# A recurrent attention kernel: keys and queries in three rounded passes, the state's halves made by GpSimd

## The reference

```python
q = _phi((h @ wq + bq_).reshape(b, s, H, DH))      # phi(t) = elu(t) + 1
k = _phi((h @ wk + bk_).reshape(b, s, H, DH))
v = (h @ wv + bv_).reshape(b, s, H, DH)
kv = jnp.einsum('bshd,bshm->bhdm', k, v)
z = 1.0 / (jnp.einsum('bshd,bhd->bsh', q, k.sum(axis=1)) + 1e-06)
att = jnp.einsum('bshd,bhdm,bsh->bshm', q, kv, z).reshape(b, s, d)
h = _ln(h + att @ wo + bo_, g1_, be1_)
y = jax.nn.gelu(h @ w1 + c1_, approximate=False) @ w2 + c2_
h = _ln(h + y, g2_, be2_)
```

## Time and profile before

| | |
|---|---|
| median of 3 runs | 879.8 us (879.21 to 880.77) |
| the profiled execution's own time | 876.81 us |
| its span | 875.1 us |
| TensorE busy | 835.1 us (95%), weight load 772.6 (88%) |
| VectorE busy | 799.0 us (91%) |
| ScalarE busy | 716.4 us (82%) |
| GpSimd busy | 394.6 us (45%) |
| mean granted clock | 0.973 |
| chain that ended last | PE 83%, DVE 10%, issue 3%, ACT 3% |

### The profile page before, as it was taken

The page is one execution under the profiler, slowest core; times in us unless marked ns, Lnnn a source line. Parts: engine busy times, 40 slices in busy tenths (PEclk is TensorE's granted clock), DMA queues, the critical chain, the costliest instruction groups (busy, mean ns, idle before and its releaser), DMA issues.

```text
span 875.1 us, 19581 instructions
## 1 busy us (share of the span) xinstructions
PE 835.1 (95%) x6170; PEld 772.6 (88%) x6170; DVE 799.0 (91%) x2698; ACT 716.4 (82%) x1271; POOL 394.6 (45%) x355
## 2 busy tenths in 40 slices
PE   6799999999999999999999999999999999988876
PEld 5598999999999999999999999999999999877663
DVE  6989999998899989999899989989899989999998
ACT  3589999989998899989998899989998889756443
POOL 5244454445445454445445455454545455432113
PEclk9899999999999999999999999999999999999885
DMA  4300101010010101010010101010010000000002
GB/s 145 88 1 2 43 1 35 1 43 2 1 34 2 43 2 34 2 43 1 1 34 2 43 2 34 1 43 1 2 34 1 2 1 1 17 10 1 1 0 98
DMA packets 26265, 18.79 MB, mean 21 GB/s; under 512 B 4354, under 2 KB 22195, under 8 KB 26164
## 3 DMA queue, kind: packets, MB, share of 16 engines
q1 hardware_dynamic: 25300, 16.95, 6.8%
q10 hardware_dynamic: 864, 0.59, 0.2%
HBM read 15.43 MB, written 2.10 MB: 20 GB/s over the span
## 4 chain that ended last, share of the span: by engine, by line
PE 83%; DVE 10%; issue 3%; ACT 3%; DMA 0%; ACTq 0%; DVEq 0%
PE down_ps L742 23%; PE att_ps L706 7%; PE small_ps L676 6%; PE k_ps L661 6%; PE q_ps L668 6%; PE up_ps L732 5%; PE up_ps L734 5%; PE up_ps L733 5%; PE t_ps L651 3%; PE t_ps L713 3%; PE up_ps L697 3%; PE small_ps L684 2%; PE k_ps L732 2%; PE k_ps L734 2%; PE small_ps L685 2%
## 5 line engine op out<-in xcount | busy, mean ns | idle before, releaser
L742 PE MATMUL down_ps<-w_use,hid 128*128 128x128 f32 x2048 | 263.5, 278 | 0.7 <-ACT hid L845 0.7
L742 PEld LDWEIGHTS down_ps<-w_use,hid 128*128 128x128 f32 x2048 | 247.6, 195 | 1.9 <-ACT hid L845 1.1
L1005 POOL TENSOR_TENSOR res_ffn<-z_tm,g_ffn 128x512 f32<-128x512 f32 x64 | 102.1, 1595 | 216.3 <-DVE z_tm L983 216.3
L995 POOL TENSOR_TENSOR res_att<-z_tm,g_att 128x512 f32<-128x512 f32 x64 | 82.6, 1291 | 204.7 <-DVE h L948 204.7
L845 ACT ACTIVATE hid<-up_ps 128x512 f32<-128x512 f32 x192 | 113.7, 592 | 20.5 <-PE up_ps L734 12.1
L960 DVE BATCH_NORM_STATS2 st<-h 128x6 f32<-128x128 f32 x512 | 108.9, 274 | 0.1
L900 ACT ACTIVATE z_tm<-h,shift,rstd 128x128 f32<-128x128 f32 x224 | 92.4, 483 | 0.7
L1008 POOL TENSOR_TENSOR res_ffn<-res_ffn,ffn_row 128x512 f32<-128x512 f32 x64 | 85.5, 1335 | 5.0
L732 PE MATMUL up_ps<-z_hi,w_hi 128*128 128x512 f32 x192 | 86.8, 452 | 0.3 <-DVE z_lo L988 0.3
L894 ACT ACTIVATE z_hi<-t_ps 128x512 fp32r<-128x512 f32 x64 | 38.1, 596 | 58.1 <-PE t_ps L713 58.1
L1058 DVE SCALAR_TENSOR_TENSOR q_ks<-q_elu,small_ps 128x512 f32<-128x512 f32 x64 | 43.9, 686 | 43.6 <-PE small_ps L685 43.0
(11 more groups left out here) (188 smaller groups left out, 1891.7 us busy)
## 6 DMA issues: line engine op xcount, KB each, us to landing
raw_w<-in_L_attn_W SPq DMA_DIRECT2D x15, 256.0 KB, 4.2
out_y<-gate_tm SPq DMA_DIRECT2D x8, 256.0 KB, 2.2
bias_bc<-in_L_attn_c SPq DMA_DIRECT2D x7, 256.0 KB, 4.5
x_tm<-in_L_attn_x SPq DMA_DIRECT2D x3, 512.0 KB, 6.6
raw_rows<-in_L_attn_be SPq DMA_DIRECT2D x15, 64.0 KB, 4.2
raw_g<-in_L_attn_g SPq DMA_DIRECT2D x14, 64.0 KB, 3.1
x_tm<-in_L_attn_x SPq DMA_DIRECT2D x2, 256.0 KB, 3.3
raw_rows<-in_L_attn_bo SPq DMA_DIRECT2D x8, 64.0 KB, 3.9
```

The costliest lines, as they stand in the source:

```text
L742: last = nc.tensor.matmul(down_ps[:, t, :], hid[:, j, t * P:(t + 1) * P], w2_use[:, j, :], start=(j == 0), stop=(j == FC - 1))
L1005: nc.gpsimd.tensor_tensor(res_ffn[:, b % 2, :, :], z1_tm[:, :, :], g_ffn[:, :].unsqueeze(1).to_broadcast([P, TT, D]), ALU.mult).then_inc(s ...
```

## The change

Keys and queries of one unit share one matmul with 256 columns, keys left and queries right: the weights stand in the order K, Q (`w_kq`), the loads of weights and biases change places accordingly, and the result goes to `kq_ps`, two PSUM banks with two tiles each. The product is made as in the up matmuls, of rounded halves: three fp32r passes per tile, 12 per unit, for the 4 + 4 float32 matmuls of before. Since the second bank is also the place of the third up chunk, that chunk waits for `q_elu_s` as well, and the keys' phi on VectorE waits for `qrel`.

The halves of the state, `zq_hi` and `zq_lo`, are made by GpSimd from `z_fm` (one buffer now) at the head of its period, ahead of both residuals. To have the state earlier, TensorE transposes it before attention, and ScalarE copies it before the second norm. For the first two units ScalarE and VectorE make the halves from PSUM. `pool_qk` splits the weights into halves likewise. `pool_res_ffn` has a further wait on `tk`.

```diff
-        q_ps = ps("q_ps", [P, TT, D])
-        k_ps = ps("k_ps", [P, TT, D])
+        kq_ps = ps("kq_ps", [P, TT, 2, D])
+        k_ps, q_ps = kq_ps[:, :, 0, :], kq_ps[:, :, 1, :]
...
         def pool_qk(pool, l):
             pool.wait_ge(s["fold_a"], l)
-            pool.wait_ge(s["qproj"], l * SEQS)
-            pool.wait_ge(s["kproj"], l * SEQS)
+            pool.wait_ge(s["kqproj"], l * SEQS)
             pool.sem_inc(s["pool_waited"], 1)
-            nc.gpsimd.tensor_copy(w_qk[:, :], fold_att[:, 0:2 * D]).then_inc(s["qk_ready"], 1)
+            nc.gpsimd.tensor_copy(w_kq_hi[:, :], fold_att[:, 0:2 * D]).then_inc(s["qk_ready"], 1)
+            pool.wait_ge(s["qk_ready"], l * 2 + 1)
+            nc.gpsimd.tensor_tensor(w_kq_lo[:, :], fold_att[:, 0:2 * D], w_kq_hi[:, :].bitcast(F32),
+                                    ALU.subtract).then_inc(s["qk_ready"], 1)
...
-        def pe_k(pe, u, b):
-            pe.wait_ge(s["zfm"], u + 1)
+        def pe_kq(pe, u):
+            pe.wait_ge(s["zq_lo_s"], u + 1)
             if after_first(u):
                 pe.wait_ge(s["kphi"], u)
-            if is_unit(u - 3):
-                pe.wait_ge(s["gelu"], (u - 3) * FC + 3)
-            for t in range(TT):
-                last = nc.tensor.matmul(k_ps[:, t, :], z_fm[:, b % 2, t * P:(t + 1) * P], w_qk[:, D:2 * D], start=True, stop=True)
-            last.then_inc(s["kproj"], 1)
-
-        def pe_q(pe, u, b):
-            if after_first(u):
                 pe.wait_ge(s["q_elu_s"], u)
             for t in range(TT):
-                last = nc.tensor.matmul(q_ps[:, t, :], z_fm[:, b % 2, t * P:(t + 1) * P], w_qk[:, 0:D], start=True, stop=True)
-            last.then_inc(s["qproj"], 1)
+                if t == 2 and is_unit(u - 3):
+                    pe.wait_ge(s["gelu"], (u - 3) * FC + 3)
+                to = kq_ps[:, t, :, :].rearrange("p w d -> p (w d)")
+                nc.tensor.matmul(to, tile(zq_hi, t), w_kq_hi[:, :], start=True, stop=False)
+                nc.tensor.matmul(to, tile(zq_hi, t), w_kq_lo[:, :], start=False, stop=False)
+                last = nc.tensor.matmul(to, tile(zq_lo, t), w_kq_hi[:, :], start=False, stop=True)
+            last.then_inc(s["kqproj"], 1)
...
                 if j == 2:
                     pe.wait_ge(s["kphi"], keys)
+                    pe.wait_ge(s["q_elu_s"], keys)
...
             if ffn:
                 pe_down(pe, p - 2, (3,))
-            if att:
-                pe_att(pe, p)
             if state:
                 if ln1:
                     pe.wait_ge(s["z1lo_s"], p)
                 pe_state_transpose(pe, p + 2, (b + 2) % SEQS)
+            if att:
+                pe_att(pe, p)
...
+        FIRST = 2
+
+        def act_state_copy(act, u):
             act.wait_ge(s["t2_ps"], u + 1)
-            if after_first(u) and after_first(u - 1):
-                act.wait_ge(s["qproj"], u - 1)
-                act.wait_ge(s["kproj"], u - 1)
-            nc.scalar.activation(z_fm[:, b % 2, :], t_ps[:, :], ACT.Identity).then_inc(s["zfm"], 1)
+            act.wait_ge(s["zq_lo_s"], u)
+            nc.scalar.activation(z_fm[:, :], t_ps[:, :], ACT.Identity).then_inc(s["zfm"], 1)
+
+        def pool_state_split(pool, u):
+            pool.wait_ge(s["zfm"], u - FIRST + 1)
+            pool.wait_ge(s["kqproj"], u)
+            pool.sem_inc(s["pool_waited"], 1)
+            nc.gpsimd.tensor_copy(zq_hi[:, :], z_fm[:, :]).then_inc(s["zq_hi_s"], 1)
+            pool.wait_ge(s["zq_hi_s"], u + 1)
+            nc.gpsimd.tensor_tensor(zq_lo[:, :], z_fm[:, :], zq_hi[:, :].bitcast(F32), ALU.subtract).then_inc(s["zq_lo_s"], 1)
...
             if is_unit(p - 1):
                 nc.scalar.preload_act_table_set("gelu_and_others")
-            if ln2 and not (isinstance(p, int) and is_final(p - 3)):
+            if state:
+                if p + 2 < FIRST:
+                    act_state_hi_first(act, p + 2)
+                else:
+                    act_state_copy(act, p + 2)
+            if ln2 and not is_final(p - 3):
                 act_norm2(act, p, (b - 3) % SEQS)
             if between:
                 between()
-            if state:
-                act_state_copy(act, p + 2, (b + 2) % SEQS)
...
             pool.wait_ge(s["z1n"], TT * (u + 1))
+            pool.wait_ge(s["tk"], min(u + 3, UNITS))
             nc.gpsimd.tensor_tensor(res_ffn[:, b % 2, :, :], z1_tm[:, :, :], g_ffn[:, :].unsqueeze(1).to_broadcast([P, TT, D]),
                                     ALU.mult).then_inc(s["t1a"], 1)
...
         def pool_period(pool, l, b):
             p = l * SEQS + b
             in_use = not isinstance(l, int) or l > 0
+            if is_unit(p + 1) and p + 1 >= FIRST:
+                pool_state_split(pool, p + 1)
...
         def dve_k_phi(dve, u):
             dve.wait_ge(s["tk"], u + 1)
+            dve.wait_ge(s["qrel"], u + 1)
```

More of the change, by code:

```diff
@@ L58, in build @@
         z_tm = sb("z_tm", [P, SEQS, TT, D])
-        z_fm = sb("z_fm", [P, 2, S])
+        z_fm = sb("z_fm", [P, S])
+        zq_hi = sb("zq_hi", [P, S], F32R)
+        zq_lo = sb("zq_lo", [P, S], F32R)
         vec_rows = sb("vec_rows", [4 * L, D])
@@ L84, in build @@
         row_sum = sb("row_sum", [P, 2, D])
-        w_qk = sb("w_qk", [P, 2 * D])
+        w_kq_hi = sb("w_kq_hi", [P, 2 * D], F32R)
+        w_kq_lo = sb("w_kq_lo", [P, 2 * D], F32R)
         w_v = sb("w_v", [P, D])
@@ L137, in build @@
         down_flat = down_ps[:, :, :].rearrange("p t d -> p (t d)")
-        q_flat = q_ps[:, :, :].rearrange("p t d -> p (t d)")
+        kq_bank = tuple(kq_ps[:, 2 * i:2 * i + 2, :, :].rearrange("p t w d -> p (t w d)") for i in range(2))
         names = """const_ready raw_a0 raw_b0 raw_w0 raw_r0 raw_wo0 raw_w20 vec_in ffn_vec_in row_in cols_ps cols_ready lv_ready ffn_cols_ps ffn_cols_ready
@@ L145, in build @@
             row_s qk_ready wv_ready wo_ready gatt_ready gffn_ready w2_ready
-            t2_ps zfm kproj krel kexp tk kphi qproj qrel qexp q_elu_s
+            t2_ps zfm zq_hi_s zq_lo_s kqproj krel kexp tk kphi qrel qexp q_elu_s
             g_ps_s g_sb_s kv_ps_s blk_s kvo_ps_s kvo_sb q_ks_s den_s den_e_s rden_s qn qn_ps qn_fm
@@ L714, in pe_z1_transpose @@
             last.then_inc(s["t1_ps"], 1)
-        up_bank = (up_ps[0][:, :], up_ps[1][:, :], k_ps[:, :, :].rearrange("p t d -> p (t d)"), up_ps[0][:, :])
+        up_bank = (up_ps[0][:, :], up_ps[1][:, :], kq_bank[1], up_ps[0][:, :])
         def pe_up(pe, u, keys, chunks):
@@ L825, in pe_period @@
                     pe.wait_ge(*read)
-                pe_z1_transpose(pe, p - 1, p + 2 if state or not isinstance(p, int) else UNITS)
+                pe_z1_transpose(pe, p - 1, (p + 2 if state else UNITS) - FIRST)
             if att:
@@ L901, in act_norm2, with act_state_hi_first, dve_state_lo_first @@
                                      bias=shift[:, i:i + 1]).then_inc(s["z2n"], 1)
-        def act_state_copy(act, u, b):
+        FIRST = 2
+        def act_state_copy(act, u):
             act.wait_ge(s["t2_ps"], u + 1)
-            if after_first(u) and after_first(u - 1):
-                act.wait_ge(s["qproj"], u - 1)
-                act.wait_ge(s["kproj"], u - 1)
-            nc.scalar.activation(z_fm[:, b % 2, :], t_ps[:, :], ACT.Identity).then_inc(s["zfm"], 1)
+            act.wait_ge(s["zq_lo_s"], u)
[7 more added lines that the diff above has]
+            nc.gpsimd.tensor_tensor(zq_lo[:, :], z_fm[:, :], zq_hi[:, :].bitcast(F32), ALU.subtract).then_inc(s["zq_lo_s"], 1)
+        def act_state_hi_first(act, u):
+            act.wait_ge(s["t2_ps"], u + 1)
+            if u > 0:
+                act.wait_ge(s["kqproj"], u)
+            nc.scalar.activation(zq_hi[:, :], t_ps[:, :], ACT.Identity).then_inc(s["zq_hi_s"], 1)
+        def dve_state_lo_first(dve, u):
+            dve.wait_ge(s["zq_hi_s"], u + 1)
+            if u > 0:
+                dve.wait_ge(s["kqproj"], u)
+            nc.vector.tensor_tensor(zq_lo[:, :], t_ps[:, :], zq_hi[:, :].bitcast(F32), ALU.subtract).then_inc(s["zq_lo_s"], 1)
         def act_period(act, l, b, between=None, behind_keys=None):
@@ L1101, in dve_q_elu @@
                 dve.wait_ge(s["qn"], u)
-            nc.vector.scalar_tensor_tensor(q_elu[:, :, :], q_e[:, :, :], -1.0, q_ps[:, :, :],
+            nc.vector.scalar_tensor_tensor(q_elu[:, :, :], q_e[:, :, :], -1.0, q_ps,
                                            ALU.add, ALU.max).then_inc(s["q_elu_s"], 1)
@@ L1226, in _ @@
                 load_x(1, 2)
-                for i, v in enumerate((bq, bk, bv)):
+                for i, v in enumerate((bk, bq, bv)):
                     sp.dma_start(b_row[:, i * D:(i + 1) * D], v[0:1, :]).then_inc(s["raw_b0"], 16)
@@ L1349, in _ @@
                 pe_down(pe, last - 1, (2,))
-                pe_z1_transpose(pe, last, UNITS)
+                pe_z1_transpose(pe, last, UNITS - FIRST)
                 pe_expert_up(pe, 1)
```

53 lines of the change are left out of this document (29 added, 24 removed).

## The result

The changed kernel takes **996.3 us** (median of 4 runs, 987.75 to 997.28) where the kernel before takes 879.5 on the same chip: a ratio of 1.130 (95% interval 1.124 to 1.137). The profiled execution took 995.65 us, its span is 993.9. The forecast was 915, and slower; so the sign was right and the size was three times too small: +117 us for +35, outside the range.

What follows compares the result with a forecast made beforehand. TensorE bounds the middle, VectorE the last layer; the change makes a 12.6 us GpSimd-VectorE loop. Six full layers 31, first and last layers' ten periods 3, start 1.3: +35 us, 915 us; own range 900 to 935, wider range 865 to 938.

Steps and rivals of the forecast that it cites:

- Keys and queries: On TensorE, 12 rounded 256-column passes at 0.116 us replace 16 f32 instructions of 1.79 us: gain 0.40 us a period.
- The state's transposes and ScalarE's order: Transposes ahead of attention wait for z_lo, 0.23 us a period on TensorE; ScalarE's reordering costs nothing.
- z_fm earlier, and up chunk 2 waiting for q_elu: ScalarE's earlier copy and TensorE's added wait both cost nothing, hidden under those engines' own work.
- GpSimd's row and m_r: GpSimd's queued work ends at T+7.67, holding VectorE's m_r wanted at T+6.74: period 12.6 us, a loss of 0.59.
- The floor pass: VectorE's keys pass, now clear of GpSimd, falls from 1.30 to 0.42 us, gaining 0.88 off the loop.
- The layer's extra GpSimd work stands in the same row: att_row, w_v, ffn_row and the weights' split on GpSimd add an estimated 2.6 us a layer.
- The weights for keys and queries were called in time: GpSimd's zq_lo ends at T+2.4, before TensorE uses the weights at T+4.19.
- I take zero: In four VectorE-bound periods at the end, the floor pass's 3.5 us gain cancels against locks elsewhere: no net change.
- the hidden row: Rival: GpSimd's row ends in time or m_r comes first, so TensorE's 11.84 us period stands: 867 us; chance 0.2.
- the partial case: Rival: m_r slips through or only some periods collide, 12.1 to 12.3 us a period, 880 to 900 us; chance 0.13.
- the passes at the price of 512 columns: Rival: TensorE's 256-column passes cost as much as 512, a 13.2 us period; within the worse case, chance 0.1.
- that zq_hi takes 1.27 us, or that the reciprocal waits too: Rival on GpSimd or VectorE: 0.5 to 0.66 us more a period, 944 to 953 us; within the worse case, chance 0.1.

Runs made afterwards that it cites:

- e9: The kernel with weights ahead and FFN residual first, with VectorE's fold matrices moved ahead of the keys' floor pass: 886.71 us.
- e8: e9 with two GpSimd waits in the last layer, keeping its state split and attention residual apart from VectorE's affine passes: 877.26 us.
- e10: e8 with TensorE's attention product again ahead of the state's transposes, as in the kernel before the change: 874.96 us.
- e4: The kernel with weights ahead and FFN residual first, with VectorE's q_elu ahead of the last affine passes in the last layer: 897.23 us.
- e7: The changed kernel with GpSimd's FFN residual left without its addition of ffn_row, one pass less: 951.08 us (one run).

## Why the prediction was right in sign and wrong in size

From the changed kernel's 996.3 us, each edit on top of the one before it:

| edit | us | gain |
|---|---|---|
| the change | 996.3 | |
| weights ahead in the row (e1) | 941.2 | 55 |
| FFN residual clear of m_r (e2) | 894.2 | 47 |
| fold matrices clear of GpSimd (e9) | 886.7 | 7.5 |
| last layer's affine passes clear of it (e8) | 877.3 | 9.4 |
| attention first (e10) | 875.0 | 2.3 |

**Keys and queries**: right. Half of a 512-column pass was taken, 0.116 us, and 0.118 was measured (343.98 to 345.16); the other bound, 0.23, is near what the pass costs at half the clock (0.21). The Trainium skill, "VectorE: DVE Perf Modes", section on the TRN2 errata, would have it at 0.109, as an estimate from its 6 + N cycles. The measured step decides.

**The state's transposes and ScalarE's order**: right as a mechanism, mis-sized. 0.23 us a period was taken; the edit taken back (e8 to e10) is worth 1.04 us a middle layer, 0.13 a period. z_fm earlier, and up chunk 2 waiting for q_elu, were costed at nothing; for the latter e4 bears that out, though it waits 9.8 us in the list.

**GpSimd's row and m_r**: right, and not by luck: counted from z1's transposes (321.46), zq_hi began 3.91 us later for 3.87 in the forecast, the row ended 11.09 later for 11.03, over m_r, and the plain period came out at 12.58 us for 12.6. Clearing m_r (e2) brought that period to 11.81. That the whole gain of e2, 47 us, is near 0.76 x 64 = 49 is in part chance: a middle layer gained 6.9 us, w_o's wait included, the last layer only 0.7. e7 shows the loop from another side. The floor pass fell to 0.42 us as laid out. The Trainium skill's "SBUF — State Buffer", section "Who interferes with whom", has a VectorE instruction with two SBUF inputs and a GpSimd instruction that reads SBUF exclude each other, the one issued first winning. The rows agree: m_r began 0.48 after GpSimd's pass and ended with it.

**The step that failed** is "The layer's extra GpSimd work stands in the same row", with its 2.6 us a layer. The work that it names takes 3.0 us a layer, near the estimate, but it was added to the period as if it delayed m_r alone; and w_use, whose wait is the longest (3.41 us), is not in its list at all. What was not asked is who waits for each copy. Three of them are wanted by TensorE, whose products have fixed places in the period; behind the new row the copies end after these. The weights for keys and queries were called in time by the end of zq_lo, which is the unit's half, not the layer's: w_kq_lo stands behind res_att. And the stalls of 3.4 us, and all but one of those of 2.2, were followed by work at half clock, for which the sum had no term (the one of 1.62 us ahead of 343.76 was not: its passes step by 0.118). Together this was 8.1 us a layer, 55 in all: with the weights in time (e1) a middle layer takes 104.54 us, near the forecast's 103.4.

**The second step that failed** is "I take zero" for the ends. The forecast knew from the earlier trace rows that two of VectorE's operations on SBUF, the floor pass and the small product, stand while GpSimd works, and applied it to those two kinds alone. The fold matrices (0.42 and 0.39 us before, 1.2 after) and the last layer's passes are of the same kind, and a longer GpSimd row fell on them: 17 us by e9 and e8. Against the kernel before, e10 still loses 5.2 us up to unit 8's copy and 6.3 in the last layer; their cause is open.

**The rivals**: the hidden row (867), the partial case (880 to 900) and the passes at the price of 512 columns are all refuted for this kernel; that zq_hi takes 1.27 us, or that the reciprocal waits too, is refuted by their 0.61 and 0.55. None of them had weights that come late.

## What to carry to other kernels

When work is put at the head of an in-order queue, list everything that stands behind it, the once-a-layer copies too, and write beside each who waits for it and when: a copy of 0.3 us that TensorE wants costs more than a pass of 1.3 that nobody waits for. Give GpSimd's long rows a window of the period in which VectorE reads PSUM, and move VectorE's operations of the kinds listed first below out of that window; here the five moves of order and place together, with no instruction less, took 121 us off. And a stall on the list of waits is the price of what it names only if the next wait in line does not take it over, as g_sb's did in e4.
